# Second graph layer of a GNN kernel: sums of a group accumulated in two PSUM banks and copied by ScalarE a step later, queries in two rounded parts

## The reference, cut to what matters

```
qkv = (h @ W_qkv + b_qkv).reshape(n, 3, H, DH)          # H = 8 heads of DH = 32
score = einsum('ehd,ehd->eh', q[dst], k[src]) * SCALE
mx = segment_max(score, dst);  ex = exp(score - mx[dst])
denom = segment_sum(ex, dst);  attn = ex / denom[dst]
h_new = segment_sum(attn[:, :, None] * v[src], dst)
```

## Time and profile before

| | us |
|---|---|
| median of three executions (lowest, highest) | 2130.21 (2125.19, 2136.06) |
| profiled execution, first to last instruction | 2134.3 |
| `project_qkv`, about | 1144 to 1241 |
| `attention_edges`, first gather | 1243.6 |
| `attention_edges`, first and last product L1910 | 1251.6, 1857.3 |
| next block begins | 1900.2 |

### The profile page before, as it was taken

How to read it: one execution, slowest core, us unless ns; L and a number is a source line. 1 busy time by engine, 2 the same in 40 slices (tenths; PEclk the granted TensorE clock), 3 DMA queues, 4 the chain that set the end, 5 groups by cost and what they waited for, 6 DMA issues and landing times. The chain is left out here.

```text
span 2134.3 us, 41549 instructions
## 1 busy us (share of the span) xinstructions
PE 1761.5 (83%) x10388; PEld 1537.1 (72%) x10389; DVE 1539.6 (72%) x2788; ACT 1070.3 (50%) x2353; POOL 1160.5 (54%) x1169
## 2 busy tenths in 40 slices
PE   3699999999999989828973868888888888866278
PEld 3499999999999979728972756666666766645267
DVE  5388888888888845643545849899999898847622
ACT  1677777777777726403420145445455454316133
POOL 0376666666666601462443457777777777512112
PEclk7799999999999989758996989999999999867579
DMA  3443333333333312133323566666666666524310
GB/s 96 133 121 111 104 108 108 104 107 108 105 106 108 98 31 80 69 124 98 119 75 98 193 185 189 189 188 188 193 191 186 190 187 188 148 65 141 115 38 29
DMA packets 132538, 267.55 MB, mean 125 GB/s; under 512 B 24030, under 2 KB 75888, under 8 KB 132407
## 3 DMA queue, kind: packets, MB, share of 16 engines
q0 software_dynamic: 63456, 191.61, 30.7%
q1 hardware_dynamic: 68534, 73.21, 11.2%
q10 hardware_dynamic: 416, 1.18, 0.2%
HBM read 225.34 MB, written 42.50 MB: 125 GB/s over the span
## 5 line engine op out<-in xcount | busy, mean ns | idle before, releaser
L319 POOL DMA_INDIRECT e_rows<-h_table,e_idx x440 | 453.4, 1030 | 214.1 <-issue 106.3
L1740 POOL DMA_INDIRECT a_rows<-kv_table,a_idx x440 | 476.1, 1082 | 135.8 <-issue 128.9
L619 PE MATMUL e_w<-w2h,e_hidl 128*128 128x256 f32 x880 | 247.7, 304 | 2.9 <-DVE e_msg L704 2.9
L589 PE MATMUL e_agg<-e_msg,e_hot 128*128 128x256 f32 x880 | 246.1, 402 | 0.0
L1822 PE MATMUL a_q<-q,a_spread 128*128 x880 | 233.7, 407 | 6.5 <-ACT a_spread L1782 6.3
L620 PE MATMUL e_w<-w2l,e_hidh 128*128 128x256 f32 x880 | 226.4, 280 | 0.0
L1853 PE MATMUL a_agg<-a_rows,x 128*128 128x264 f32 x880 | 226.2, 402 | 0.0
L704 DVE TENSOR_TENSOR e_msg<-e_w,e_rows 128x1024 f32<-128x1024 f32 x110 | 134.7, 1224 | 93.4 <-PE e_w L623 93.4
L1775 ACT ACTIVATE a_apart<-iota_n,dst_rel 128x128 f32<-128x128 f32 x440 | 140.6, 391 | 112.9 <-PE a_agg L1853 112.8
L1822 PEld LDWEIGHTS a_q<-q,a_spread 128*128 128x128 f32 x880 | 166.2, 199 | 38.9 <-issue 12.8
L1853 PEld LDWEIGHTS a_agg<-a_rows,x 128*128 128x128 f32 x880 | 168.2, 200 | 24.7
(11 more groups left out here) (456 smaller groups left out, 4221.4 us busy)
## 6 DMA issues: line engine op xcount, KB each, us to landing
e_ea<-in_eaT SPq DMA_DIRECT2D x220, 64.0 KB
m_rows<-expert_rows SPq DMA_DIRECT2D x32, 272.0 KB, 2.7
e_rows<-h_table,e_idx POOLq DMA_INDIRECT x440
a_rows<-kv_table,a_idx POOLq DMA_INDIRECT x440, 3.7
q_ab<-expert_out SPq DMA_DIRECT2D x50, 128.0 KB, 3.3
kv_table<-q_kv SPq DMA_DIRECT2D x25, 256.0 KB, 2.2
u_stage<-in_m_w SPq DMA_DIRECT2D x16, 256.0 KB
x<-in_x SPq DMA_DIRECT2D x1, 3200.0 KB, 13.9
```

What stands on the lines that cost most here:

```text
L319: c.nc.gpsimd.indirect_dma_start(out=rows[:, g.slot8, j, :], out_offset=None, in_=table, in_offset=bass.IndirectOffsetOnAxis(ap=idx[:, g.s ...
L589: last = mm(bank(wins[j]), hot[:, g.slot4, t, :], msg[:, g.slot4, t, :], start=False, stop=False, skip_group_check=True)
L619: mm(w, hidl[:, g.slot, cols[k]], w2h[:, k, :], start=(k == 0), stop=False)
L1740: nc.gpsimd.indirect_dma_start(out=rows[:, g.slot * IG + j, 0:2 * D], out_offset=None, in_=c.kv_dram, in_offset=bass.IndirectOffsetOnAxis( ...
```

## The change

1. In the loop, both banks of `a_agg` are kept filled. A window has the bank of its parity, and its sum grows there over groups (no product begins with `start`). Two products of two columns with zeros (`a_none`) are issued ahead of a group's sums, in the place of L1848. ScalarE copies both banks to `c.sums` after each group, in the step after (`keep`, two copies of 264 numbers); VectorE's add L1890 is gone. GpSimd clears a spare piece of x, and ScalarE copies it into the banks, before the loop.
2. TensorE adds a group's messages one step later (`SUM = LAG + 1`), as the last thing in a step. The ring of one-hots has 12 groups, the ring of rows still ten.
3. `q` is split in `project_qkv` into a part rounded to fp32r (ScalarE) and the rest (GpSimd, ten windows behind). The loop does two fp32r products for each tile in the place of one in fp32. `c.sums` and the parts share their memory, a window apart, and `c.sums` is no longer cleared.
4. VectorE's order: the message stands after the product of the step; at place 2 behind the scores' reduction. The rescaling is at place 3, on the PSUM bank, from a copy `a_grown` that ScalarE makes.
5. The small products of a chunk stand ahead of the last tile's query products, and `tails` ahead of the sums.

```diff
-                nc.gpsimd.memset(c.sums[:, :, :], 0.0).then_inc(s_clr, 1)
+                def query_low(t):
+                    need(pool, s_pg, (s_qh, t + 1))
+                    high, low = c.qhl[:, t, 0:D], c.qhl[:, t, D:2 * D]
+                    nc.gpsimd.tensor_tensor(low, q[:, t % GT, :], high.bitcast(F32), ALU.subtract).then_inc(s_ql, 1)
+                def query_high(t):
+                    need(act, s_ag, (s_s, t + 1))
+                    nc.scalar.copy(c.qhl[:, t, 0:D], q[:, t % GT, :]).then_inc(s_qh, 1)
...
+    SUM = LAG + 1
+    HR = 12
+    bank = lambda w: ap[:, bass.ds(w & 1, 1), 0:DM].rearrange("p a d -> p (a d)")
...
+                act.wait_ge(s_zero, 1)
+                for p in range(2):
+                    nc.scalar.copy(ap[:, p, 0:D], zero[:, :])
+                    nc.scalar.copy(ap[:, p, D:DM], zero[:, 0:H]).then_inc(s_zero, 1)
+                def keep(a, j, w):
+                    need(act, s_ag, (s_agg, a.n + 1), (s_acc, a.n * JG + j))
+                    nc.scalar.copy(window(c.sums, w)[:, 0:DM], bank(w)).then_inc(s_acc, 1)
...
+                def add_group(m, both):
+                    wins = both >> 1, (both + 1) >> 1
+                    need(pe, None, (s_msg, m.n + 1), (s_acc, m.n * JG), *([(s_rs, 2 * m.chunk + 2)] if m.place == 0 else []), own=True)
+                    for w in [p for p in previous] + [wins[0]]:
+                        mm(other(w)[:, 0:2], none[:, :], none[:, 0:2], start=True, stop=False, skip_group_check=True)
+                    previous[:] = [wins[1]]
+                    for j in range(IG):
+                        last = mm(bank(wins[j // CT]), hot[:, hots(m, j), :], rows[:, m.slot * IG + j, D:ROW], start=False, stop=False, skip_group_check=True)
+                    last.then_inc(s_agg, 1)
...
-                            last = mm(qp[g.pair][:, j * D:(j + 1) * D], spread[:, g.pair, j, :], window(c.q, wins[j // CT]), start=True, stop=True)
+                            if j == IG - 1:
+                                chunk_rows(i, ch)
+                            both_parts = window(c.qhl, wins[j // CT])
+                            mm(qp[g.pair][:, j * D:(j + 1) * D], spread[:, g.pair, j, :], both_parts[:, 0:D], start=True, stop=False)
+                            last = mm(qp[g.pair][:, j * D:(j + 1) * D], spread[:, g.pair, j, :], both_parts[:, D:2 * D], start=False, stop=True)
...
-                        to = c.sums[:, bass.ds(w, JG), :]
-                        v.tensor_tensor(to, to, ap[:, :, 0:DM], ALU.add).then_inc(s_acc, 1)
+                def rescale(i, ch):
+                    w = ahead.take(i.step, "crossing", ch * (CH // IG))
+                    need(dve, s_dg, (s_gn, ch + 1), (s_acc, (i.n - SUM) * JG))
+                    to = bank(w)[:, 0:D].rearrange("p (h d) -> p h d", h=H)
...
```

More of the change, by code:

```diff
@@ L1748, in step @@
                 def step(at):
                     i = at(0)
[L1750 to L1764, removed]
+                    a = at(-SUM - 1)
@@ L1765, in step @@
+                    if real(a):
+                        wins = item_windows(act, c, a.n)
+                        keep(a, 0, wins[0])
                     g = at(4)
@@ L1803, in step @@
                     ch = i.chunk - 1
-                    if i.place == 0 and closed(ch):
-                        need(pe, None, (s_sc, min(i.n, NIG) if isinstance(i.n, int) else i.n), (s_rs, 2 * ch), own=True)
-                        tr(scT, sc[:, at(-1).cslot, :, :].rearrange("p t h -> p (t h)"), c.ident[:, :]).then_inc(s_sT, 1)
-                    if i.place == 1 and closed(ch):
-                        need(pe, None, (s_cs, 2 * ch + 2), own=True)
-                        mm(carries[:, 0:2 * (CH + 1)], c.heads_of_row[:, :], c.carried[:, :, :].rearrange("p a t -> p (a t)"), start=True, stop=True).then_inc(s_ca, 1)
+                    m = at(-SUM)
+                    sums = ahead.take(i.step, "sums", m.n) if real(m) else None
                     g = at(1)
@@ L1838, in step @@
                         for j in range(IG):
-                            last = tr(hT[:, j * P:(j + 1) * P], hot[:, h.slot * IG + j, :], c.ident[:, :])
+                            last = tr(hT[:, j * P:(j + 1) * P], hot[:, hots(h, j), :], c.ident[:, :])
                         last.then_inc(s_ht, 1)
+                    if i.place == 0 and closed(ch):
+                        need(pe, None, (s_en, ch + 1), own=True)
+                        mm(tails, c.rows_of_head[:, :], ends[:, :, :].rearrange("p a t -> p (a t)"), start=True, stop=True).then_inc(s_tl, 1)
                     if i.place == 2 and closed(ch):
@@ L1845, in step @@
                     if real(m):
[L1847 to L1858 removed]
+                        add_group(m, sums)
                 pe.wait_ge(s_none, 1)
[L1860 removed]
+                pe.wait_ge(s_zero, 3)
+                rounds(pe, step, 4, SUM + 1, Edges)
             @block.vector
@@ L1881, in step @@
                 def step(at):
                     i = at(0)
+                    m = at(-LAG)
                     ch = i.chunk - 1
-                    a = at(-LAG - 1)
-                    if real(a):
-                        w = ahead.take(i.step, "sums", a.n)
-                        need(dve, s_dg, (s_agg, a.n + 1), (s_acc, a.n), *([(s_rs, 2 * a.chunk + 2)] if a.place == 0 else []))
-                        to = c.sums[:, bass.ds(w, JG), :]
-                        v.tensor_tensor(to, to, ap[:, :, 0:DM], ALU.add).then_inc(s_acc, 1)
```

185 lines of the change are left out of this document (112 added, 73 removed).

## The result

The changed kernel takes 2137.7 us (median of 20 runs, 2121.57 to 2153.1), the kernel before 2128.39 beside it (20 runs). The ratio is 1.0051, 95% interval 1.0031 to 1.0070: slower by 0.5%, where 1.4% faster was forecast. In its 20 runs the time falls as the mean granted TensorE clock rises: 0.893 to 0.897 in the four fastest (up to 2127.2), 0.876 to 0.884 in the four slowest (from 2146.1). The kernel before shows the same relation in its runs beside the first experiments (0.912 at 2121.0, 0.904 at 2135.9), so this alone doesn't say what causes what.

The account below looks back on a forecast made before the run. GpSimd's gather issuing was taken to bound the loop. Loop -31, clock +3, loop start +1 and tail -6 gave -33 us: 2101 from the profiled 2134.3, 2097 from the median, taken as 2098; 8-in-10 range 2071 to 2128.

Parts of the forecast that it names:

- Loop bound by the gathers: Loop: GpSimd's gather issuing sets the pace, 20.0 us a chunk without stalls; VectorE follows with almost nothing to spare.
- the prediction's formula: Loop: a gather beginning under a message stalls for the message's end less its own start less 0.13 us.
- A chunk of 21.2: Loop: a chunk takes 21.2 us, 1.2 of it stalls, in place of 22.33; -31 us over 27.25 chunks.
- TensorE from 19.4 us a chunk to "about 16": Loop: fp32r queries and smaller zero products cut TensorE's work per chunk; nothing waits for it, so worth 0.
- The clock ... I allow +3 us: Loop: with less work and idle pieces TensorE drops to its lower clock more often; +3 us, 0 if slack absorbs it.
- The third rival: Loop: TensorE at the lower clock carries a chunk's chain, 23.3 us a chunk, +27 us, 2152 in all; chance 11%.
- The ring is ten deep and the sums lag seven, so 0: Loop: gathers wait for sums of ten groups before, now a step later; expected cost 0.
- Tail: After the last product: steps fall from 6.3 to about 4.8 us; -6 us net, bounds 0 to -11.
- Seven groups remain: Tail: seven groups are left after the last product, saving 7 x 1.5 = 10.5 us before the closing chunks' waits.
- `project_qkv` at 0 to 3: Before the loop: 25 roundings on ScalarE and 25 subtractions on GpSimd, which loses its clearing; 0 us, at most 3.
- The stall rule: Loop: a gather beginning under a two-SBUF-input message stands still until it ends; one that began first is not touched.

Follow-up runs that it names:

- f4: Changed kernel with one exact fp32 query product per tile, a ring of 12, VectorE's second copy of sums in the tail and fp32 zeros: 2116.8 us, ratio 0.9955.
- g2: f4 with its message cut into two halves of two tiles each: 2117.8 us, ratio 0.9954.
- h1: f4 with two useless 128x512 products ahead of each group's sums in the tail: 2114.8 us, ratio 0.9943.
- e4: Kernel before with VectorE's addition L1890 cut to the denominators' columns, numerators left out: 2105.7 us, ratio 0.9905.
- e3: Changed kernel with one fp32 product per tile of queries, high part alone, in place of two fp32r ones: 2126.7 us, ratio 0.9999.
- g1: Changed kernel with four fp32r products per tile of queries in place of two, the low part added three times: 2126.4 us, ratio 0.9996.
- e2: Changed kernel with a ring of 12 groups of rows in place of 10, the queries' high part taken twice: 2130.9 us, ratio 1.0014.
- h3: h1 with the message in halves and the useless products from one step earlier: 2108.1 us, ratio 0.9909.
- f2: Kernel before with each query product as two fp32r products, the high part taken twice: 2128.4 us, ratio 1.0002.

## Why the prediction was wrong

- **Loop bound by the gathers: right where the clock is kept.** At full clock and with twelve slots they stand end to end (f4, g2, h1), and of 89 gathers over 1.0 us in the trace before (1300:1830) 82 began under the message, 6 under a scan, and the prediction's formula gives each of the 82 stalls to 0.02 us. A cut of 44 us on VectorE gave 16 (e4).
- **A chunk of 21.2: mis-sized, then overtaken.** Where the clock is kept and slots don't wait (f4), it is 20.0 for the gathers and 1.6 of stalls, 21.6; the term had 1.2. That is -13 to -15 us in the loop in the place of -31 (e3 592.7, g1 591.8, f4 590.2, from 605.7).
- **TensorE from 19.4 us a chunk to "about 16": the first failed step.** It is 459.19 x 16 / 384 = 19.1. Part of that is clock: one chunk of 23.8 us holds two sums that take 1.3 to 1.7 us longer. Part is the queries: the eight fp32r products take about 1.3, not 1.05. Behind the fp32 sums the second of them begins 0.31 after the first, where inside the row they are 0.12 apart. And part is the zeros, which the forecast took for shorter. From the first of them to the first of the sums are 0.57 us in the median at full clock. The single one of 264 columns that they replace took 0.21 to 0.23 before, as in the first fence; the second is from the changed kernel:

```profile
1494.20 0.37 PE L1848 MATMUL a_agg<-a_none 128*128 128x264 f32 x1
1494.41 1.94 PE L1853 MATMUL a_agg<-a_rows,x 128*128 128x264 f32 x8
```

```profile
1808.90 0.38 PE L1921 MATMUL a_misc<-a_diag,a_first 8*128 8x8 f32 x2
1809.21 0.52 PE L1862 MATMUL a_agg<-a_none 128*128 128x2 f32 x2
1809.77 2.04 PE L1865 MATMUL a_agg<-a_rows,x 128*128 128x264 f32 x8
1811.45 0.47 PE L1898 MATMUL a_q<-q_parts,a_spread 128*128 x1
...
1812.48 0.27 PE L1899 MATMUL a_q<-q_parts,a_spread 128*128 x1
```

  In g1, behind the one-hots' transposes, the same two take 0.22 in the median. Register instructions for the bank's address stand ahead of each of the two, so the columns aren't the cost; that these instructions are is likely, not shown.

- **"The clock ... I allow +3 us": the step that decided.** g1 and e3 put it at about 15 in the loop. The third rival (11%) described it: sums of places 3 and 0 at the lower clock, 23.3 a chunk; measured 23.7. It held in nine of the 26 chunks, and the loop ended at +1.6, not at the rival's +27. The rows for it were there. The Trainium skill (TensorE: Matmul & The Clock Gate, "HAM oscillation — how this bites in real kernels") says that such falls come again in every round of a loop whose products have idle gaps. The trace agrees in direction, with both falls in nine of 26 chunks and a clock of 0.92 in the place of 0.98. With the stalls' 16 to 18 us and the clock's 12 beyond the 3 allowed, the loop's missing 30 us (-28 forecast, +1.6 measured) are accounted for.
- **"The ring is ten deep and the sums lag seven, so 0": wrong.** Gathers go three groups ahead: 3 + 7 = 10, the whole ring, so the slack is what is left of one step. The forecast counted the lag and not the lead. It is worth some 7 us (e2), inside the clock's 15.
- **Tail: wrong by 16 us.** Priced at two copies of 0.37, the hand-over takes 1.95 us (the copies 0.75 apart, with their waits on both sides), so a step is 6.26 in the mean and not 4.8; and the delay adds a step. "Seven groups remain" was counted from the order before; with a step's delay there are eight.
- **`project_qkv` at 0 to 3: wrong, -4.5**; see below.
- **The stall rule against the Trainium skill's inference** (SBUF — State Buffer, "Who interferes with whom"): the section infers that a two-input tensor_tensor does not stop the making of descriptors. The rows stay against it: the 17 traces whose message has two inputs in SBUF all show stalls under it, the longest 0.88 to 1.08 us, and in g2 they shorten with the instruction (0.42 us in the mean in the place of 0.55).

What stays open: the rest of f4's tail, how much of h3's lead over h1 is real, and what the lower clock alone would cost the kernel before.

## What to carry to other kernels

Work taken off an engine that isn't the bound can make things worse if that engine's clock depends on being busy: look for what is queued behind its next long piece at the lower clock, and price that chain before calling the saving free. Slack in a ring is its depth less lag and lead together; a pipeline's extra step is paid once more in the tail, where nothing hides it.

## What the runs showed of the hardware

GpSimd's clearing of `sums` (kernel before) stopped VectorE. GpSimd, then VectorE, whose instruction of this kind takes 0.41 at other times:

```profile
1211.78 5.82 POOL L1461 MEMSET sums<- 128x6864 f32 x1
```
```profile
1212.30 0.42 DVE L1524 BATCH_NORM_STATS2 norm_stat<-x 128x6 f32<-128x256 f32 x1
1212.64 5.11 DVE L389 TENSOR_SCALAR q_xn<-x,norm_mv,norm_rstd 128x256 f32<-128x256 f32 x1
1217.67 0.41 DVE L1533 TENSOR_TENSOR q<-q_p,q_b 128x256 f32<-128x256 f32 x1
```

It ends when the clearing ends: 4.7 us lost on VectorE, which was on this block's path. The other two kernels that clear (e4, f2) show it too, with 5.25 and 5.13 us, and none of the other 15 does. I had priced the clearing at nothing, because GpSimd idles after it. Without it the block is 4.5 us shorter in the changed kernel. The split of the queries isn't the reason, since f4 has neither the split nor the clearing: from the start of `project_qkv` to the first gather it takes 94.2 us, the changed kernel 95.6, the kernel before 99.2.

And work of no use can pay: in g1, 39 us more of products in a stretch of 520 came with a rise of the clock from 0.92 to 1.00 and of the pace by 2.7% (382 gathers against 372).
